# State-space stage: VectorE takes both products with C once in four steps, in place of once in eight, in the last batch

## The reference

```python
def step(state, xs):
    d_t, B_t, C_t, u_t = xs
    dA = jnp.exp(d_t[..., None] * A)
    state = state * dA + (d_t * u_t)[..., None] * B_t[:, None, :]
    y_t = jnp.einsum('ben,bn->be', state, C_t)
    return (state, y_t)
...
y = y + D[None, :, None] * u
y = y * jax.nn.silu(z)
```

## Time and profile before

| what | us |
|---|---|
| median of 3 runs | 1829.29 (1825.97 to 1833.02) |
| the profiled execution | 1830.79 |
| its span, first to last instruction | 1828.3 |
| state-space stage, until the last VectorE instruction | about 507 |
| POOL's row of the page (whole span) | 683.9 busy, 37% |
| DVE's row of the page | 1364.8 busy, 75% |

### The profile page before, as it was taken

One profiled execution on the slowest core, in us unless ns is written; L12 is line 12 of the kernel. 1 busy time (PEld: TensorE's weight loads), 2 busy tenths in 40 slices (PEclk: granted clock), 3 DMA queues, 4 the chain that ended last, 5 costly groups with the idle time before them and its releaser, 6 DMA issues. The chain is left out here.

```text
span 1828.3 us, 20886 instructions
## 1 busy us (share of the span) xinstructions
PE 1490.6 (82%) x6523; PEld 615.0 (34%) x6523; DVE 1364.8 (75%) x2030; ACT 911.1 (50%) x1201; POOL 683.9 (37%) x462
## 2 busy tenths in 40 slices
PE   5997998976742873599889988998899379999997
PEld 1333433332221421333243334324432133343433
DVE  6989999899985854589678946866793788657453
ACT  4766565663330100447654763685376254546453
POOL 3999999999924235100100010001001033333332
PEclk7899999998875997789999999999999689999998
DMA  7455455555487544300000000000000720000000
GB/s 235 127 154 147 141 146 141 153 148 142 123 196 183 122 111 156 121 1 1 1 1 1 1 1 1 1 1 1 1 1 1 157 65 1 23 1 24 1 24 23
DMA packets 65210, 131.52 MB, mean 72 GB/s; under 512 B 11328, under 2 KB 11328, under 8 KB 64336
## 3 DMA queue, kind: packets, MB, share of 16 engines
q1 hardware_dynamic: 53056, 104.07, 20.0%
q0 software_dynamic: 7168, 25.17, 6.0%
q10 hardware_dynamic: 4880, 0.95, 0.3%
HBM read 134.11 MB, written 12.85 MB: 80 GB/s over the span
## 5 line engine op out<-in xcount | busy, mean ns | idle before, releaser
L363 POOL TENSOR_TENSOR ssm_dBu<-ssm_du,ssm_BC 128x1024 f32<-128x1024 f32 x128 | 303.7, 2378 | 17.5 <-DVE ssm_du L399 17.5
L258 PE MATMUL ssm_psY<-ssm_hC,ident 128*128 128x512 f32 x512 | 254.2, 627 | 43.8 <-POOL ssm_hC L370 29.6
L1459 DVE TENSOR_REDUCE att_next_mx<-att_next_ring 128x1 f32<-128x512 f32 x384 | 241.9, 684 | 32.7 <-PE att_next_ring L1209 31.0
L327 ACT ACTIVATE ssm_dA<-ssm_delta,ssm_negA 128x512 f32<-128x512 f32 x256 | 165.4, 682 | 169.7 <-DVE ssm_hC L419 168.3
L1363 ACT ACTIVATE att_next_Pr<-att_next_psT 128x1024 f32<-128x1024 f32 x192 | 186.2, 1023 | 88.5 <-PE att_next_psT L1233 87.9
L1597 POOL TENSOR_TENSOR mlp_both<-mlp_first,mlp_third 128x512 f32<-128x512 f32 x88 | 124.7, 1417 | 256.7 <-DVE mlp_first L1799 175.4
L1799 DVE SCALAR_TENSOR_TENSOR mlp_first<-mlp_psQ,mlp_s_gu,mlp_first 128x512 f32<-128x512 f32 x176 | 131.5, 749 | 110.0 <-ACT mlp_first L1691 90.2
L1473 POOL TENSOR_TENSOR X<-X,att_bout 128x512 f32<-128x512 f32 x12 | 15.9, 1351 | 491.2 <-SPq L1120 491.2
L464 DVE TENSOR_TENSOR_SCAN ssm_dA<-ssm_dA,ssm_dBu 128x512 f32<-128x512 f32 x144 | 174.6, 1223 | 20.8 <-ACT ssm_dA L327 14.2
L1623 PE MATMUL mlp_psQ<-mlp_xh,mlp_Vgu 128*128 128x512 f16 x352 | 141.4, 402 | 50.3 <-ACT mlp_Vgu L1679 27.6
L258 PEld LDWEIGHTS ssm_psY<-ssm_hC,ident 128*128 128x128 f32 x512 | 96.8, 198 | 192.7 <-issue 100.1
(11 more groups left out here) (313 smaller groups left out, 2479.8 us busy)
## 6 DMA issues: line engine op xcount, KB each, us to landing
ssm_BC<-bc_rows SPq DMA_DIRECT2D x128, 512.0 KB, 4.8
moe_W<-in_masksT POOLq DMA_DIRECT2D x32, 512.0 KB, 7.8
mlp_words<-in_gate_upT SPq DMA_DIRECT2D x32, 176.0 KB, 7.4
X<-in_x SPq DMA_DIRECT2D x4, 1024.0 KB, 10.7
rows<-moe_XP SPq DMA_DIRECT2D x4, 1024.0 KB, 27.8
moe_XP<-results SPq DMA_DIRECT2D x4, 1024.0 KB, 9.1
out_x<-X SPq DMA_DIRECT2D x4, 1024.0 KB, 4.3
mlp_Wd<-in_downT SPq DMA_DIRECT2D x8, 352.0 KB, 15.3
```

Source lines behind the costliest of these rows:

```text
L258: nc.tensor.matmul(psY[:, w, :], ident[:], hC[:, w, g % RC, :], start=False, stop=(n == DS - 1)).then_inc(summed, 1)
L327: nc.scalar.activation(dA[:, q % RA, :], delta[:, b % 2, e, :], ACT.Exp, scale=negA[:, e, n:n + 1]).then_inc(dA_done, 1)
L363: nc.gpsimd.tensor_tensor(dBu[:, g % RB], du[:, b % 2, hh * W:(hh + 1) * W, :], BC[:, g % RING, 0, :].unsqueeze(1).broadcast_to([P, W, S]) ...
L1459: nc.vector.tensor_reduce(mx[:, m % 3, qt, row_order(j)], bank(("score", i)), AX.X, ALU.max).then_inc(maxed, 1)
```

## The change

In the last batch (g from `LAST` = 96) every fourth pass is whole, in place of every eighth: 99, 103, 107, 111, 115, 119, 123 and 127. Passes 103, 111, 119 and 127 were whole before; 99, 107, 115 and 123 are new. Four products of 128 x 512 move from POOL to DVE, and the counts that the waits use are reckoned by a new function `wholes(n)`, the number of whole passes among the first n.

```diff
-    FULL = 8
+    FULL, FULL_LAST = 8, 4
+    LAST = TOTAL - PER
...
         def whole(g):
 
-            return g % FULL == FULL - 1
+            every = FULL if g < LAST else FULL_LAST
+            return g % every == every - 1
+
+        def wholes(n):
+
+            return min(n, LAST) // FULL + max(n - LAST, 0) // FULL_LAST
 
         def await_second(eng, g):
 
-            fulls = (g + 1) // FULL
+            fulls = wholes(g + 1)
...
                         elif whole(g):
-                            pe.wait_ge(hC_both, (g + 1) // FULL)
+                            pe.wait_ge(hC_both, wholes(g + 1))
                         else:
-                            pe.wait_ge(hC_done[1], g + 1 - (g + 1) // FULL)
+                            pe.wait_ge(hC_done[1], g + 1 - wholes(g + 1))
...
                         elif q >= RA and whole(g - RA // W):
-                            act.wait_ge(hC_both, (g - RA // W + 1) // FULL)
+                            act.wait_ge(hC_both, wholes(g - RA // W + 1))
...
-                        pool.wait_ge(hC_done[1], g - RB + 1 - (g - RB + 1) // FULL)
+                        pool.wait_ge(hC_done[1], g - RB + 1 - wholes(g - RB + 1))
```

## The result

The changed kernel took 1823.21 us (median of 21 runs, 1819.89 to 1830.71), the kernel before 1830.27 us (21 runs). The ratio is 0.9967 with a 95% interval of 0.9958 to 0.9976: 4.4 to 7.7 us less. (The two medians lie 7.1 us apart; the ratio stands for 6.0.) By my bound of 0.5% that is "the same", and it is 2 us more than the forecast 4.0 us.

What follows compares the result with a forecast made beforehand. POOL was taken as the bound near the last batch's end, DVE following. Gains of 1.17 + 2.84 = 4.0 us take the profiled 1830.79 to 1826.8, or 1825.3 us from the median 1829.29; range 1821.5 to 1830.5.

Steps and rivals of the forecast that it cites:

- What bounds the stage: Last batch of the first stage: POOL is the bound near the end, DVE following at 3.54 us a pass.
- First stretch: Last batch until add_delta(3, 1): without product 99 POOL stops earlier, so add_delta ends earlier; gain 1.17 us.
- rival A: At add_delta(3, 1): it gets in at once when product 104 ends; gain 6.3 us, 1823.0 us; chance 0.16.
- Second stretch: Product 105 to the end: three products less, 3.69 us, minus 0.85 of POOL waits; gain 2.84 us.
- Does VectorE become the bound?: From pass 105's start: DVE's passes and extras total 72.9 us, which just fits, ending at 498.5.
- Rival B: DVE takes the later gain if gates or dA come 3 us late; 1828.1 us; chance 0.10.
- The tail: End of the batch: PE's queue runs 4.56 us from product 125's end, now 495.8 instead of 499.8, to 500.4.
- rival C: PE's clock is slow over the last five products: 4.56 us become 9.4, +0.9 us, 1830.2 us; chance 0.07.
- rival D: Transfers of B and C land in 7.0 us: eight shortened weighs wait 1.3 us each, +6.4 us, 1835.7; chance 0.02.
- some 0.3 us in the worst case: Eight more weighs 5.85 us after product g - 5: transfers landing within 6.1 us stay hidden but for this.
- The rule that disagreed with a row: Shared SBUF port: whichever engine issues first holds it; fits add_delta at j = 27, not the 5.81 us at j = 8.
- the likeliest case: Whole kernel: the forecast of 4.0 us less, 1825.3 us, own range 1822.5 to 1828; chance 0.60.

Runs made afterwards that it cites:

- every2: Changed kernel with every second pass of the last batch whole, moving eight more products from POOL to VectorE; 1826.45 us, ratio 0.9981.
- sync_after: Changed kernel plus a wait making VectorE reach add_delta(b, 1) when POOL starts the product of pass 8, in all batches; 1823.80 us, ratio 0.9956.
- after_again: The changed kernel run and profiled once more with no edit; 1823.98 us, ratio 0.9963.
- only_late: Kernel before with only passes 107, 115 and 123 made whole in addition, 99 as before; 1826.95 us, ratio 0.9977.
- shift3: Kernel before with its whole passes at 3, 11, 19, ... in place of 7, 15, 23, ...; 1829.14 us, ratio 0.9989.
- all4: Changed kernel with every fourth pass whole in all four batches, moving twelve more products to VectorE; 1819.45 us, ratio 0.9938.
- sync_before: Kernel before plus a wait making VectorE reach add_delta(b, 1) when POOL starts the product of pass 8, in all batches; 1831.62 us, ratio 1.0003.
- before: The kernel before the change, unedited, in its first profile; profiled execution 1830.79 us.
- only_99: Kernel before with only pass 99 made whole in addition, 107, 115 and 123 as before; 1825.52 us, ratio 0.9973.
- after_look3: The changed kernel with no edit, a third profile; single run, 1821.41 us.

## Why the prediction was right, and where it wasn't

**What bounds the stage** (right). POOL's products lay on the path: each stretch got shorter when they went, and VectorE alone became the bound when more went (`every2`).

**First stretch, 1.17 us** (the mechanism held, the outcome mostly didn't). Measured as it was reckoned, from the first gate to product 105 (35.00 us before), it gained 1.18 us in `sync_after` and 0.78 in the first profile, which has the 0.41 us for a transfer in it. VectorE's wait for ACT ahead of pass 102 fell from 1.17 to 0.57 us and took up the second product of pass 99, as said. I reckoned that pass 102 and add_delta's start stay where they are, and that product 104 starts at about 421.0. In `after_again` add_delta starts 26.87 us after the gate, before 26.86; product 104 starts 26.82 after it, forecast 26.8. What failed is the next step: "I go by the rows, as it was so in all four batches at j = 8". Those four rows all had add_delta issued well before the product; the change moves POOL against it by 1.2 us, as I had written under rival A, and at the new place it is let in. The stretch gains 3.52 us in that form (31.48 in `after_again`), as rival A had it (3.5), and not 1.17. I gave rival A 0.16; three of four profiles of the changed kernel show it, so it should have been the likeliest. In the form that I expected, the profile without a wait for a transfer (`sync_after`, which has an added wait) has the sum: 4.01 us.

**Second stretch, 2.84 us** (right). Measured 2.86 in the first profile and in `only_late` (78.59 from product 105 to the next stage, before 81.45), 2.85 in `after_again`, 2.83 in `sync_after`. The waits at 108 and 116 were 0.37 and 0.33 us, forecast 0.35 and 0.45.

**Does VectorE become the bound?** It just fits, as said: VectorE went from 427.21 (pass 105) to the end of pass 127's second product at 500.2 with no wait, 72.9 us forecast and 73.0 measured. Rival B's price wasn't paid.

**The tail and rival C.** PE's last run was 4.56 us at the full clock in all four profiles of the changed kernel. Rival C did not occur in them, but it isn't far-fetched: in `shift3` the same ten records took 6.82 us at a granted clock of 0.66.

```profile
500.03 6.82 PE L258 MATMUL ssm_psY<-ssm_hC,ident 128*128 128x512 f32 x10 [1.00 <-POOL ssm_hC L370]
```

**Transfers, rival D.** There was a wait of 0.41 us for one in one of the four profiles of the changed kernel, and one of 0.38 in `only_late`. Both stand ahead of weigh(99). That isn't one of the eight weighs that the change shortens: up to pass 99 both kernels run the same instructions, and the distance from product 94 to weigh(99) is 5.85 us before as well. So the change didn't make these waits, none of the eight has one in any profile, and "some 0.3 us in the worst case" remains untested. (The rival's 1.3 us a weigh doesn't follow from its own numbers either: 7.0 - 5.85 is 1.15, 9.2 us in all.) What I had not seen is that such a wait can act twice: it also moves add_delta's phase. The one profile of the changed kernel that has it is the one with the long form, and its last batch is 2.7 us longer than the others'. That the wait is what tipped it fits the phases, but wasn't tried by itself.

**The rule that disagreed with a row.** Rival A reckoned 6.3 us by letting add_delta in at the next end of a POOL instruction, and `after_again` has 6.37. The Trainium skill, "SBUF — State Buffer", section "Who interferes with whom", says that the order of issue decides which of the two engines blocks the other. By that rule the short rows come out (`after_again`: in after product 104, weigh(107) held up), and the long ones in the same place don't, neither before nor in `sync_after`. Here the measurements decide: both happen.

**The sum.** Forecast 1825.3, measured 1823.2 and 1824.0, in the range of 1821.5 to 1830.5 and in the likeliest case's own of 1822.5 to 1828. But the interval of the ratio (4.4 to 7.7 us) leaves out 4.0. It holds the 6.4 of the short form, and it also holds the 4.0 of the long form with some 2 us of the last stage on top. Three of four profiles have the short form, so the number was in part near by luck: the likeliest case was rival A's. How many of the timed runs have either form, and which last stage, isn't shown.

## What to carry to other kernels

When a change shifts two engines against each other, a contended instruction whose cost was read at one phase has no fixed price: look up every instance of it at other phases, and take the cheap and the dear form both as live cases. Work taken off the busier of two nearly level engines pays by its own length only until another is level; count that engine's whole chain first, and the third engine's too (in `all4` it was PE). A gain of a few tenths of a per cent needs both: profiles that say where, and more than one of them.

## What the runs showed of the hardware that I had not expected

The same add_delta (128 x 1024, two inputs in SBUF) took 1.23 us alone, 1.9 to 2.6 when it was let in at the end of a running GpSimd instruction, and 4.6 to 8.8 when GpSimd's instructions went ahead of it until GpSimd had nothing ready to run; it then always ended about 1.1 us after GpSimd stopped.

The last stage (MLP) came in two lengths: 401.1 to 402.2 us in five profiles (both of the kernel before, `sync_before`, `sync_after`, `only_late`), 398.1 to 399.4 in the other nine (all four of the changed kernel among them, but also `shift3`). They differ in how long PE's clock was low. Between 130 and 385 us into that stage it was at half (1.2 GHz) for 13.7 us in each of the five, and for 6.8 or 10.2 us in the nine. In `before` the longer stretch lies 314 us into the stage, in the other four at about 145 us. Windows of 10 us, before and after, 314 us into the stage (columns as in the earlier trace rows), with a granted clock of 0.66 in the one and 0.83 in the other:

```profile
1741.23:1751.23 10.00, 7.46 (x19) 3.04 (x19) 6.88 (x10) 5.05 (x7) 3.34 (x4) 0.66 0.28 106
```

```profile
1739.20:1749.20 10.00, 8.00 (x23) 3.32 (x24) 6.30 (x9) 4.58 (x7) 4.12 (x3) 0.83 0.28 105
```

One such window isn't enough to tell the two lengths apart. At 140 us `before` has 0.83 and the changed kernel 1.00, but `only_99` has 0.83 there as well, and its stage is one of the short ones (399.1 us):

```profile
1567.23:1577.23 10.00, 6.87 (x24) 2.29 (x25) 8.52 (x14) 7.06 (x11) 3.44 (x3) 0.83 0.28 105
```

```profile
1563.43:1573.43 10.00, 6.86 (x24) 2.36 (x23) 8.51 (x14) 6.99 (x11) 3.61 (x3) 0.83 0.28 105
```

In the short form's profile `after_look3` the span is 9.0 us shorter than before: 6.4 from the last batch, 2.0 from this stage, 0.8 from attention, and 0.2 longer elsewhere. What makes the slow stretch longer or shorter wasn't tried, and the change doesn't settle it: `shift3`, with one whole pass in eight, has the short stage, and `sync_after` the long one.
